# Gate logits as eight more columns of the output product, routing one step forward, a new prologue

## The reference, cut to what matters

```python
x = x + tanh(g_xattn[0]) * xattn(layernorm(x), ctx, ctx, W_qkv, b_qkv, W_out, b_out)   # x: (32, 128, 128) f32
x = x + tanh(g_ffn[0])   * moe(layernorm(x), Wg, W1, b1, W2, b2)

# xattn: 16 heads of width 8; softmax(q k^T / sqrt(8)) v, then @ W_out + b_out
# moe: tokens = x.reshape(-1, 128), 8 experts, capacity C = T // 8 = 512
logits = tokens @ Wg
gates = softmax(logits)
idx = argmax(gates)                       # one expert for each token
mask1 = one_hot(idx)
locations1 = cumsum(mask1, axis=0) - 1    # place in the expert's queue, in token order
mask1 = mask1 * (locations1 < C)          # beyond its capacity a token is dropped
out = gate * (relu(expert_in @ W1 + b1) @ W2 + b2), put back in token order
```

## Time and profile before

| | us |
|---|---|
| median of 3 runs | 356.81 |
| the three runs | 356.81, 358.24, 352.88 |
| the profiled execution's own time | 352.81 |
| its span (first to last instruction) | 351.0 |

### The profile page before, as it was taken

How to read it: one execution, slowest core, us unless ns; L and a number is a source line. 1 busy time by engine, 2 the same in 40 slices (tenths; PEclk the granted TensorE clock), 3 DMA queues, 4 the chain that set the end, 5 groups by cost and what they waited for, 6 DMA issues and landing times.

```text
span 351.0 us, 8166 instructions
## 1 busy us (share of the span) xinstructions
PE 261.1 (74%) x2960; PEld 169.0 (48%) x2960; DVE 201.8 (57%) x696; ACT 158.5 (45%) x357; POOL 173.4 (49%) x202
## 2 busy tenths in 40 slices
PE   0348698888996995996896888969331899999920
PEld 0124445545654654654654555635220366777720
DVE  6244649778895895568687597932320144544520
ACT  7253376865764763564674456551010332322100
POOL 5336724757179179238728625070462005555572
PEclk9999999999998998589899699995555699999985
DMA  2984765615244235208217111074014225664300
GB/s 79 294 222 110 229 183 149 182 32 162 64 115 129 66 91 152 63 3 230 51 29 209 43 56 64 5 200 76 30 51 130 71 64 162 186 200 142 89 37 21
DMA packets 48536, 39.26 MB, mean 112 GB/s; under 512 B 9619, under 2 KB 44072, under 8 KB 48497
## 3 DMA queue, kind: packets, MB, share of 16 engines
q1 hardware_dynamic: 44784, 28.67, 30.5%
q0 software_dynamic: 3712, 10.07, 8.6%
HBM read 13.72 MB, written 12.65 MB: 75 GB/s over the span
## 4 chain that ended last, share of the span: by engine, by line
POOL 26%; issue 26%; PE 22%; ACT 8%; DVE 7%; DMA 5%; SPq 2%; POOLq 1%; ACTq 0%; DVEq 0%
POOL rec_dram L1002 7%; POOL out_dram L1056 6%; POOL rs L982 4%; PE O L489 3%; PE X L418 3%; ACT prob L623 2%; ACT xn L615 2%; DVE negm L734 2%; POOL rec L988 2%; PE S L460 2%; POOL rec L990 2%; PE X L412 2%; PE TS L561 2%; PE X L435 2%; DMA qp<-parts_q 2%
## 5 line engine op out<-in xcount | busy, mean ns | idle before, releaser
L734 DVE TENSOR_REDUCE negm<-S 128x4 f32<-128x512 f32 x128 | 81.8, 680 | 27.5 <-PE S L460 26.5
L623 ACT ACTIVATE prob<-TS 128x512 f32<-128x512 f32 x128 | 72.0, 589 | 47.5 <-PE TS L475 47.3
L489 PE MATMUL O<-prob,vals 128*32 128x128 f32 x1024 | 58.1, 303 | 1.6 <-ACT oraw L632 1.6
L460 PE MATMUL S<-kp,qp 62*128 62x128 bf16 x512 | 33.5, 234 | 5.2 <-DVE negm L734 4.7
L1056 POOL DMA_INDIRECT out_dram<-fin,tok x32 | 31.3, 979 | 11.2 <-issue 11.2
L1002 POOL DMA_INDIRECT rec_dram<-rec,slot x32 | 31.8, 994 | 9.7 <-issue 9.7
L256 POOL TENSOR_TENSOR rest_k<-full_k,parts_k 128x512 f32<-128x512 f32 x7 | 8.1, 1155 | 53.4 <-ACT parts_k L606 53.4
L489 PEld LDWEIGHTS O<-prob,vals 128*32 128x32 f32 x1024 | 21.3, 113 | 21.7 <-issue 10.9
L975 POOL TENSOR_TENSOR fence_p<-pool_c 128x1 f32<-128x1 f32 x16 | 3.1, 194 | 56.7 <-DVE fin L955 34.3
L460 PEld LDWEIGHTS S<-kp,qp 62*128 62x128 bf16 x512 | 19.2, 100 | 23.5 <-issue 11.7
L475 PE MATMUL TS<-qp,kp 64*128 64x128 bf16 x512 | 28.9, 228 | 1.3 <-DMA qp<-mrow 1.3
(11 more groups left out here) (115 smaller groups left out, 513.1 us busy)
## 6 DMA issues: line engine op xcount, KB each, us to landing
kp<-parts_k SPq DMA_DIRECT2D x48, 128.0 KB
qp<-parts_q SPq DMA_DIRECT2D x48, 128.0 KB, 2.7
rec_dram<-zeros POOLq DMA_DIRECT2D x8, 516.0 KB
xr<-rec_dram SPq DMA_DIRECT2D x8, 260.0 KB, 2.9
c_sb<-in_ctx_dram SPq DMA_DIRECT2D x8, 256.0 KB, 4.4
out_dram<-rec SPq DMA_DIRECT2D x8, 256.0 KB
w1s<-in_L_ffn_W_dram SPq DMA_DIRECT2D x8, 256.0 KB, 3.1
w2s<-in_L_ffn_W_dram SPq DMA_DIRECT2D x8, 256.0 KB, 2.9
```

Source lines behind the costliest of these rows:

```text
L460: mm = nc.tensor.matmul(S[:, a, i * L:(i + 1) * L], qp[b][rows, h, t0:t0 + L], kp[b][rows, h, t0:t0 + L], start=True, stop=True)
L489: mm = nc.tensor.matmul(o_out[i * HV:(i + 1) * HV, u * L:(u + 1) * L], vals[G % 2][:, k, h, :], prob[n % 2][:, h * L:(h + 1) * L], start=( ...
L623: nc.scalar.activation(prob[n % 2][:, first:first + 4 * L], TS[:, a, :], ACT.Exp).then_inc(a_exp, 1)
L734: V.tensor_reduce(negm[n % 2][:, first:first + 4], S[:, a, :].rearrange("p (h k) -> p h k", k=L), AX.X, ALU.max, negate=True).then_inc(v_r ...
```

## The change

The logits of the second layer norm are linear in the row before it, up to a scale and a constant: with the column means taken out of Wg (`wg_c`), LN(x1) @ Wg = x1 @ wg_c / std(x1) for the differences between experts. x1 is x plus the output product, so x1 @ wg_c comes out as eight more columns: `wout_g` and `bout_g` are widened from 128 to 136 columns (their products with `wg_c`, made on PE in steps 0 and 1), and x @ wg_c is made from the transposed normalised x times its deviation `sd1` (task `xl` on PE at j = 0, `x_logits` on DVE). The argmax needs no scale; for the softmax `ldif` is multiplied by 1/std (`scaled`) when POOL has it. The transposition `nT`, its copy `xn2T`, the product `lg` and the copy `lgs` go away.

`route` moves from j = 2 to j = 0, `pos` from j = 3 to j = 1 (with 5 matmuls in place of 14), `positions` and `place` from j = 3 to j = 2; all scatters stand at j = 3 now, that of group 6 too. x's statistics, `offset1` and the transposition of x keep their steps. The prologue: the first context tile is loaded second, the later parts of x one group at a time, `kp` and `qp` are filled as they are needed (two `qp` by POOL), group 0's q is split on DVE, group 1's statistics are taken early, and the zero fill of `rec_dram` lies in steps 1 to 8.

```diff
-            third = {2: ("lg", g - 2), 3: ("pos", g - 2)}.get(j)
+            third = {0: ("xl", g), 1: ("pos", g - 2)}.get(j)
-            second = {1: ("nT", g - 2), 2: ("xT", g + 2), 3: ("q", g + 2)}.get(j)
+            second = {2: ("xT", g + 2), 3: ("q", g + 2)}.get(j)
 # sync
+            sp.dma_start(c_sb[0][:], ctx_v[:, 0:GB, :]).then_inc(c_in[0], 16)   # second transfer of all
-                if c == -7:
-                    sp.dma_start(x_sb[:, 2 * GB:, :], x_v[:, 2 * GB:, :]).then_inc(x_in[2], 16)
+                if j == 2 and 2 <= g + 3 < NG:
+                    rows = slice((g + 3) * GB, (g + 4) * GB)
+                    sp.dma_start(x_sb[:, rows, 0:D], x_v[:, rows, :]).then_inc(x_in[g + 3], 16)
 # tensor
-                elif name == "nT":
-                    pe.wait_ge(g_xn2, idx + 1)
...
-                elif name == "lg":
-                    pe.wait_ge(a_nT, idx + 1)
...
+                elif name == "xl":
+                    for k in range(GB):
+                        mm = nc.tensor.matmul(X[:, 1, k * E:(k + 1) * E], xnT[idx % 2][:, k * L:(k + 1) * L], wg_c[:],
                                               start=True, stop=True)
-                    nc.tensor.matmul(X[:, 0, 0:D], onT[(c - 5) % 2][:], wout_g[:], start=True, stop=True).then_inc(p_at, 1)
+                    nc.tensor.matmul(X[:, 0, 0:DE], onT[(c - 5) % 2][:], wout_g[:], start=True, stop=True).then_inc(p_at, 1)
 # scalar
-                if j == 1 and is_group(g - 2):
-                    G = g - 2
-                    act.wait_ge(p_nT, G + 1)
-                    nc.scalar.activation(xn2T[:], X[:, 0, :], ACT.Copy).then_inc(a_nT, 1)
 # vector
             def offset1(H):
                 dve.wait_ge(g_rs1, H + 1)
                 V.scalar_tensor_tensor(nm1[:], mv1[:, :, 0], -1.0, rs1[:, 1, :], ALU.mult, ALU.mult).then_inc(v_nm, 1)
+                V.tensor_tensor(sd1[H % 2][:], rs1[:, 0, :], rs1[:, 1, :], ALU.mult).then_inc(v_sd, 1)
+            def scaled(G):
+                dve.wait_ge(v_lraw, G + 1)
+                dve.wait_ge(g_rs2, G + 1)
+                V.tensor_tensor(ldif[:], ldif[:], rs2[:, 1, :].unsqueeze(2).broadcast_to([P, GB, E]), ALU.mult).then_inc(v_ldif, 1)
             def step(c):
+                if j == 2 and is_group(g - 2):
+                    positions(g - 2)
...
+                if j == 0 and is_group(g):
+                    x_logits(g)
+                if j == 0 and is_group(g - 2):
+                    route(g - 2)
+                if j == 1 and is_group(g - 2):
+                    scaled(g - 2)
                 if j == 2 and is_group(g - 2):
-                    logits(g - 2)
-                if j == 3 and is_group(g - 2):
-                    positions(g - 2)
-                if j == 2 and is_group(g - 2):
-                    route(g - 2)
-                if j == 3 and is_group(g - 2):
                     place(g - 2)
+                if c == -5:
+                    gathered1(1)
+                    split(dve, V, 0, 0)
+                    offset1(1)
 # gpsimd
-                if j == 0 and g - 3 == NG - 2:
-                    scatter(NG - 2)
-                for i in {-7: (0, 1), 0: (2,), 1: (3,), 2: (4,), 3: (5,), 4: (6,), 5: (7,)}.get(c, ()):
+                for i in ((c - 1,) if 0 <= c - 1 < ZEROED else ()):
                     zero_records(i)
-                if j == 3 and is_group(g - 2) and g - 2 != NG - 2:
+                if j == 3 and is_group(g - 2):
                     scatter(g - 2)
```

More of the change, by code:

```diff
@@ L110, in flamingo_kernel @@
         xn = sb("xn", [P, GB, D])
-        xnT = sb("xnT", [P, GT])
+        xnT = [sb(f"xnT{i}", [P, GT]) for i in range(2)]
         st1 = sb("st1", [P, GB, 6])
@@ L115, in flamingo_kernel @@
         nm1 = sb("nm1", [P, GB])
+        sd1 = [sb(f"sd1_{i}", [P, GB]) for i in range(2)]
         full = [sb(f"full_{s}", [P, GT]) for s in "qk"]
@@ L132, in flamingo_kernel @@
         rs2 = sb("rs2", [P, 2, GB])
-        rec = [sb(f"rec{i}", [P, GB, REC]) for i in range(3)]
-        xn2T = sb("xn2T", [P, GT])
-        lgs = sb("lgs", [P, GB, E])
+        rec = [sb(f"rec{i}", [P, GB, D + DE]) for i in range(3)]
         lmax = sb("lmax", [P, GB])
@@ L168, in flamingo_kernel @@
         s_cst, s_wqkv, s_bias, s_late = sem("s_cst"), sem("s_wqkv"), sem("s_bias"), sem("s_late")
-        s_zero, s_vset, s_tanh, s_pset = sem("s_zero"), sem("s_vset"), sem("s_tanh"), sem("s_pset")
-        x_in = [sem(f"x_in{i}") for i in range(3)]
+        s_zero, s_vset, s_tanh, s_pset, s_gain = sem("s_zero"), sem("s_vset"), sem("s_tanh"), sem("s_pset"), sem("s_gain")
+        x_in = [sem(f"x_in{i}") for i in range(NG)]
         c_in, m_in = sem2("c_in"), sem2("m_in")
@@ L346, in step @@
                     sp.dma_start(out_v[:, sl, :], rec[(g - 2) % 3][:, :, D:2 * D]).then_inc(x1_out[(g - 2) % 3], 16)
-                if loads:
+                if loads and g + 2 >= 1:
                     if g + 2 >= 2:
@@ L498, in step @@
                 at_q = {0: [t for t in groups if t[0] in ("v", "cT") or t[0] == "k" and j == 3], 1: [],
-                        2: [t for t in groups if t[0] in ("lg", "pos", "xT", "q") or t[0] == "k" and j == 2],
-                        3: [t for t in groups if t[0] == "nT"]}
+                        2: [t for t in groups if t[0] in ("xT", "q", "xl") or t[0] == "k" and j == 2],
+                        3: [t for t in groups if t[0] == "pos"]}
                 if is_batch(c):
@@ L540, in step @@
                     values(c - 3, 1, 1)
+                if c == -6:
+                    pe.wait_ge(s_wg, 16)
+                    pe.wait_ge(g_mean, 1)
+                    nc.tensor.matmul(O[:, 0, 0:E], mean_w[:], wg_sb[:], start=True, stop=True).then_inc(p_wm, 1)
+                if c == 0:
+                    pe.wait_ge(s_vset, 3)
+                    pe.wait_ge(v_wgc, 1)
+                    nc.tensor.transpose(O[:, 0, 0:P], wout_g[:, 0:D], ident)
+                    nc.tensor.transpose(O[:, 0, P:2 * P], bout_g[:, 0:D], ident).then_inc(p_wT, 1)
+                if c == 1:
+                    pe.wait_ge(v_wT, 1)
+                    nc.tensor.matmul(O[:, 0, 0:E], outT[:, 0, :], wg_c[:], start=True, stop=True)
+                    nc.tensor.matmul(O[:, 0, E:2 * E], outT[:, 1, :], wg_c[:], start=True, stop=True).then_inc(p_wl, 1)
             run_steps(step)
@@ L642, in step @@
                     exps(c - 2, 0, 1)
-                if j == 2 and is_group(g + 2):
+                if j == (2 if g + 2 else 1) and is_group(g + 2):
                     H = g + 2
@@ L652, in step @@
                         first_part(1, 0)
-                if j == 2 and is_group(g + 2):
+                if j == 2 and is_group(g + 2) and g + 2 != 0:
                     normed1(g + 2, (2, 3)).then_inc(a_xn, 1)
+                if c == -5:
+                    act.wait_ge(s_vset, 2)
+                if c == -4:
+                    act.wait_ge(s_gain, 32)
+                    nc.scalar.activation(tg[:], gains[:], ACT.Tanh).then_inc(s_tanh, 1)
                 if is_batch(c - 2):
@@ L685, in step @@
                     nc.scalar.activation(lexp[:], ldif[:], ACT.Exp).then_inc(a_lexp, 1)
-            for i in range(3):
-                nc.scalar.memzero(qp[i][:]).then_inc(a_pad, 1)
-            act.wait_ge(s_bias, 96)
-            nc.scalar.activation(tg[:], gains[:], ACT.Tanh).then_inc(s_tanh, 1)
-            act.wait_ge(s_vset, 1)
+            nc.scalar.memzero(qp[0][:]).then_inc(a_pad, 1)
             run_steps(step)
@@ L897, in step @@
+                if c == -5:
+                    gathered1(1)
+                    split(dve, V, 0, 0)
+                    offset1(1)
+                if j == 0 and is_group(g + 2) and g + 2 != 1:
                     moments1(g + 2)
-                if j == 1 and is_group(g + 2):
+                if j == 1 and is_group(g + 2) and g + 2 != 1:
                     offset1(g + 2)
-            for i in range(3):
-                V.memset(kp[i][:].rearrange("p h n -> p (h n)").bitcast(F32), ONES_B).then_inc(v_pad, 1)
```

199 lines of the change are left out of this document (119 added, 80 removed).

## The result

The changed kernel takes 350.12 us (median of 4 runs, 348.68 to 350.60), the kernel before 356.27 (4 runs, 352.88 to 358.24). The ratio is 0.985, with a 95% interval of 0.981 to 0.990: a gain, but under the 2% that count. The profiled execution took 350.32 us, with a span of 348.5 beside 351.0. The forecast was 329, with a range of 319 to 341.

The account below looks back on a forecast made before the run. No engine is full; a chain through several engines was taken to set the cycle. Terms -6 + 0 - 4 - 2 - 14 = -26, plus 1, took 352.8 to 327.8; the forecast was 329, range 319 to 341.

Parts of the forecast that it names:

- Prologue, -6: Before the first scores: earlier context tile, q split on DVE and earlier statistics save 6 us, between 3 and 9.
- The ramp, "0, at most 1 us either way": Steps 1 to 8: zero fill and x's later parts lie there now, congestion changes little, 0, at most 1 us either way.
- the +1 for new short operations: Added to the sum: 1 us for new short operations and steps 0 and 1, where PE and DVE hand over widened weights.
- the +1 for `route`: Cycle before the first scatter: `route`, now in j = 0 ahead of the next statistics, costs 1 us on DVE.
- The full cycles, 0: Steps 5 to 23: x's chain stays, PE's wait moves; three cycles gain 1 us, `route` costs 1, together 0.
- 320 rival: The cycles gain too: `sd1` not held or DVE catches up, and no cycle of 31.0; 320 us, chance 17%.
- Steps 24 to 31, -6: Last groups without x to normalise: 4 us gained in steps 24 to 27, 2 in steps 28 to 31.
- to the last row, -8: Tail up to the last output row: rows 3.0 to 3.3 us apart, the last at 241.5, 8 us earlier.
- Behind the last row, -6: Rest of the tail's 14 us: group 6's scatter is ahead, last scatter issued at 250.7 to 252.6 instead of 265.44.
- the pause costs more than it did: Rival: PE's pause in one piece of 4 to 5 us drops cycles to half clock, 13 us; 339 us, chance 20%.
- slower: Rival: PE at half clock from step 5 to the attention's end; 364 us or more, put at 370, chance 2%.

Follow-up runs that it names:

- e13: The changed kernel, unedited, run once more on another chip, without late results: 338.3 us, ratio 0.963 against the kernel before.
- e10: The kernel before, unedited, on the chip of e9, with late results: 352.8 us.
- e1: The changed kernel without its 32 indirect scatters into rec_dram (the experts then read zero records): 319.97 us.
- e16: The kernel before without its 32 scatters (the experts then read zero records): 313.1 us.
- e15: The kernel of e12 again, timed, on a chip without late results: 317.9 us, ratio 0.905 against the kernel before.
- e14: The changed kernel with x's statistics at the end of j = 3 instead of j = 0 and x's loads one group earlier: 337.6 us.
- e4: The changed kernel with `sd1` made at the end of j = 3 instead of right behind `nm` at j = 1: 348.7 us.
- e17: The changed kernel with the zero fill of rec_dram at steps -7 to -5 instead of 1 to 8: 355.5 us, ratio 1.002 against the kernel before.
- e18: The kernel of e15 with the zero fill of the kernel before (step -7 and steps 0 to 5): 337.4 us, ratio 0.953 against the kernel before.
- e9: The changed kernel, unedited, once more, with late results: 349.8 us, ratio 0.988 against the kernel before.
- e12: The changed kernel with x's statistics and `sd1` at j = 3, x's loads earlier, both roots ahead of the scatters of groups 0 to 5 at j = 0: 335.9 us.

## Why the prediction was wrong

Two steps failed. The ramp, steps 0 to 12, was put at nothing and cost 9.5 to 11.1 us. And from step 24 to the last row the forecast gained 14 us, but the result lost 3.4 there, with late results, of which no row of before shows one. On a chip without them the kernel takes 338.3 us (e13), 12 less than the result; that lies inside the range of 319 to 341, but by luck, since the loss in the ramp stood in no part of the forecast. The lengths again, us:

| kernel, late results | step 0 at | 0 to 12 | 12 to 24 | 24 to 31 | to the last row | to the end | span |
|---|---|---|---|---|---|---|---|
| before, no | 31.3 | 66.6 | 84.2 | 41.3 | 25.9 | 101.7 | 351.0 |
| e10, before, yes | 30.9 | 65.9 | 81.1 | 45.4 | 24.6 | 103.1 | 351.0 |
| after, yes | 24.7 | 77.7 | 79.8 | 44.8 | 25.8 | 95.7 | 348.5 |
| e13, after, no | 24.4 | 76.1 | 81.0 | 38.4 | 17.5 | 95.6 | 333.0 |
| e1, after, no scatters | 24.7 | 77.2 | 80.4 | 36.9 | 17.5 | 81.5 | 318.2 |
| e16, before, no scatters | 31.3 | 65.7 | 71.3 | 35.8 | 20.4 | 86.8 | 311.3 |
| e15, no | 25.3 | 73.0 | 66.7 | 38.0 | 18.9 | 95.9 | 317.8 |

*Prologue, -6:* right. The first scores come at 24.31, within the 24 to 25, instead of 30.65: -6.3.

*The ramp, "0, at most 1 us either way":* this step failed, +11.1 us in the result and +9.5 in e13 (+10.9 in e14, on the same chip). With the +1 for new short operations and the +1 for `route` the sum had 2 us at most for steps 0 to 12. I had asked only about transfers and had priced `sd1` for the full cycles, with the longest `nm` of the earlier trace rows as its bound. A held operation can be held longer than the longest one in the trace: 3.10 and 2.92 us. Of the 9.5 us e4 gives back 3.2 by step 8. Another 2 stand in step 8, where `route` met `norm2` on DVE (two of its operations took 1.06 and 1.01 us in the trace of after), which is the "+1" of the forecast at twice its size. Some 4 us stay open: PE waits for small transfers and runs at half clock from 34.2 to 47.9 (full clock before), and neither e17 nor e18 freed them.

On `sd1` the page "SBUF — State Buffer" of the Trainium skill (section "Who interferes with whom") had been cited for a hold by one operation, 1.1 us. The traces show both less and more: 0.15 us in the full cycles, where `sd1` fell in the gap ahead of POOL's next operation, 1.19 us once (at 89.35), and 3 us where a zero transfer and two operations followed each other; with the zero fill elsewhere (e17) 0.156 at most.

*The full cycles, 0:* the length of a cycle was right (26 to 27 forecast, 26.6 measured), and x's chain did stay, but not alone. Over steps 12 to 24 it was -4.4, or -3.2 in e13, since the cycle of 31.0 has no successor; the forecast had that only in its 320 rival. At j = 0 DVE's queue, `route` and the statistics, took the place of a part of the wait at `nm`: the step takes 6.8 us in e13, 5.3 before and 5.9 in e14, where the statistics are gone from it. e14 moved the one and met the other (8.8 us at j = 1); only the whole set of e15 gave 4.8 us a cycle (66.7 us for three, 81.0 in e13). DVE's wait at `nm` was forecast at 3 us or more a cycle and is 1.9 us in all in the result, 5.6 in e13 (1.23 a cycle). PE was to idle 4 to 5 us in one piece in each cycle; its longest pause in the cycle from step 12 is 2.27 us in the result, for `mrow`, and 2.35 in e13, for `at_e`.

*Steps 24 to 31, -6, and to the last row, -8:* in e13 -2.9 and -8.4, so the -6 were half, and the -8 came, though with luck: 3.0 to 3.3 us between rows were forecast for a TensorE at half clock, but e13 has 3.3, 2.8 and 2.6 at full clock, and the result at half clock 4.8, 4.0 and 3.1. Step 26's maxima start 7.0 us behind step 25's in the result (189.66 and 196.68) and 5.2 in e13; it was 9.9 (186.64 and the earlier trace rows), and 3 to 4 less were forecast. In the result +3.5 and -0.1: 14.7 us more than e13 in the same steps, with two stretches without results (behind the scatters of 202 and 228 us), and half clock behind the second for 41 us. The trace of before, on which the forecast rests, has no late result, so no step of it could price them; no rival had them either.

*Behind the last row, -6:* right, -6.0. The last scatter is issued 10.0 us after the last row, forecast 9 to 11; before it was 16.1.

*The rivals:* "the pause costs more than it did", 339, has e13's number, but not its mechanism: the cycles have a granted clock of 0.87 to 0.94, not 0.78. In "slower" a cycle wholly at half clock was put at twice the 4.3 us; from 0.94 down to 0.50 it would be 2.75 times that by the same rows. That estimate makes the rival's 370 too low.

What late results are I can't settle, nor whether the signal behind a product is late or the product's record too early. What the runs show is this. In e1, the one run without scatters on a chip that has them, none is left in the attention, and one wait of 4.8 us stays at `yb`, beside the scatters to the output. All kernels with scatters on chips A and C have them (9 traces, e9's and e10's unedited ones among them) and none of the 7 on B and D. The changed kernel is 11.5 us slower with them (349.8 and 338.3), and the kernel of e12 and e15 18 us (335.9, one execution, and 317.9). These are differences between chips; for the changed kernel the lengths above put theirs in the steps from 24 to the last row, and in the cycles from 12 to 24 it is no slower with them. For the kernel before a cost isn't shown: its medians on C and D are 355.3 and 350.2, but the execution behind the first trace, without them, and that of e10, with them, both took 352.81. Every execution that was timed was also profiled, so these runs can't say whether late results occur without a profiler.

## What to carry to other kernels

When a wait is removed, list the whole queue of each engine in that step: here the pause had three owners (PE's wait, DVE's queue, POOL's order), and the first two edits alone only handed it to the next. Do the same for the steps that fill the pipeline: they held the largest miss of this forecast. On POOL, put the short operation that others wait for ahead of transfers and wide operations: with x's statistics early and both roots ahead of the scatter the same work took 318 us instead of 338. And take a new trace of the kernel before on the chip of the result, and look at its waits and not only at its time, before explaining a missing gain by the edit.
